# The causal mask of the second key block moved from TensorE to a GpSimd select, and PV one slot later

## The reference

```
x = layernorm(hidden) * ln1_g + ln1_b                 # 32 x 256 x 128
Q, K, V = low-rank projections of x, 16 heads of 8    # each 32 x 16 x 256 x 8
scores = Q @ K^T / sqrt(8)
scores = where(causal, scores, -1e9)                  # query s sees keys t <= s
attn = softmax(scores)
ctx = attn @ V
h = hidden + ctx @ out_U @ out_V + out_b
out = x0 + h + MLP(layernorm(h)) + experts(top 2 of 9)
```

## Time and profile before

| | us |
|---|---|
| median of 3 runs | 999.45 |
| lowest, highest | 994.67, 1008.21 |
| the profiled execution | 1002.02 |
| its span | 1000.1 |

### The profile page before, as it was taken

One profiled execution on the slowest core, in us unless ns is written; L12 is line 12 of the kernel. 1 busy time (PEld: TensorE's weight loads), 2 busy tenths in 40 slices (PEclk: granted clock), 3 DMA queues, 4 the chain that ended last, 5 costly groups with the idle time before them and its releaser, 6 DMA issues. The chain is left out here.

```text
span 1000.1 us, 25308 instructions
## 1 busy us (share of the span) xinstructions
PE 956.2 (96%) x7722; PEld 742.4 (74%) x7722; DVE 698.5 (70%) x3195; ACT 533.9 (53%) x1248; POOL 428.1 (43%) x557
## 2 busy tenths in 40 slices
PE   4689999999999999999999989999999999999997
PEld 4455666666666666666666659999999999989896
DVE  5768889778777777777777745555555554558887
ACT  2663555555555555555555555555555555564442
POOL 9331221354645556454555425444444444430110
PEclk8779999999999999999999999999999999999999
DMA  9477453444554454443433032222222222248874
GB/s 243 126 233 228 164 206 110 136 137 132 156 150 131 126 151 141 130 121 105 134 107 121 30 90 72 66 66 62 66 64 65 65 65 65 73 135 232 230 214 135
DMA packets 139765, 127.12 MB, mean 127 GB/s; under 512 B 17338, under 2 KB 121908, under 8 KB 139636
## 3 DMA queue, kind: packets, MB, share of 16 engines
q1 hardware_dynamic: 116336, 68.94, 25.4%
q0 software_dynamic: 20592, 56.43, 18.0%
q10 hardware_dynamic: 2708, 0.15, 0.2%
HBM read 57.15 MB, written 42.60 MB: 100 GB/s over the span
## 5 line engine op out<-in xcount | busy, mean ns | idle before, releaser
L1441 DVE CUSTOM_DVE_ANT_0 att_masked_st<-att_m_ps,att_mask_st 128x128 bf16<-128x128 f32 (+1 forms) x1024 | 311.4, 353 | 100.1 <-PE att_m_ps L1034 52.1
L846 ACT ACTIVATE att_probs<-att_t_ps 128x512 f32<-128x512 f32 x384 | 229.0, 597 | 206.2 <-PE att_t_ps L1058 201.0
L1683 POOL DMA_INDIRECT y_scratch<-moe_y,moe_row_now x136 | 131.6, 968 | 153.8 <-DVE moe_y L1937 112.6
L664 POOL DMA_INDIRECT slot_x<-xs,att_slot_now x128 | 127.7, 998 | 151.3 <-PE att_t_ps L1058 128.4
L1931 DVE TENSOR_TENSOR moe_hidden<-moe_gate,moe_up_ps 128x352 f32<-128x352 f32 x136 | 70.9, 521 | 109.8 <-ACT moe_gate L1858 108.1
L1058 PE MATMUL att_t_ps<-att_mask_ts,att_ident_b 128*128 128x256 bf16 (+1 forms) x384 | 122.9, 320 | 0.0
L1760 PE MATMUL moe_y_ps<-w_down,moe_hidden_t 128*128 (+1 forms) x816 | 114.0, 276 | 1.7 <-DVE moe_y L1937 1.5
L1858 ACT ACTIVATE moe_gate<-moe_gate_ps 128x352 f32<-128x352 f32 x136 | 63.1, 464 | 97.2 <-PE moe_up_ps L1743 97.2
L1760 PEld LDWEIGHTS moe_y_ps<-w_down,moe_hidden_t 128*128 128x128 f32 (+1 forms) x816 | 101.8, 191 | 3.5 <-issue 3.2
L1441 DVE DVE_READ_ACCUMULATOR2_ANT att_row_max<- 128x1 f32 x1024 | 84.5, 83 | 0.1
L1057 PE MATMUL att_t_ps<-even_stack,att_k_stack 97*128 97x512 f32 x192 | 80.5, 419 | 3.6 <-DMA even_stack<-att_neg_max 3.2
(11 more groups left out here) (268 smaller groups left out, 2053.6 us busy)
## 6 DMA issues: line engine op xcount, KB each, us to landing
att_k_stack<-att_qk_parts POOLq DMA_DIRECT2D x96, 128.0 KB, 3.3
slot_x<-xs POOLq DMA_DIRECT2D x17, 516.0 KB, 3.5
xs<-slot_x SPq DMA_DIRECT2D x34, 258.0 KB, 3.0
xs<-xn_scratch SPq DMA_DIRECT2D x32, 256.0 KB
mlp_rows<-y_scratch POOLq DMA_DIRECT2D x16, 512.0 KB, 5.4
even_stack<-att_qk_parts SPq DMA_DIRECT2D x192, 32.0 KB
att_odd_stack<-att_qk_parts SPq DMA_DIRECT2D x192, 32.0 KB
first_words<-in_L_attn_hidden_states SPq DMA_DIRECT2D x8, 512.0 KB, 7.9
```

Of the source, the lines that this page charges most:

```text
L664: pool.indirect_dma_start(env["slot_x"][:], bass.IndirectOffsetOnAxis(ap=slot_now[c.parity][:, col:col + 1], axis=0), xs[c.parity][:, t, k ...
L846: act.activation(probs[:, m % PT, :], t_ps[m % 2][:], ACT.Exp).then_inc(exp_done, 1)
L1441: last = dve.tensor_tensor_reduce(out=masked_st[m % 2][:, part], in0=m_ps[m % 2][:, part], in1=mask_st[:, SEQ - width:], scale=1.0, scalar ...
L1683: pool.indirect_dma_start(env["y_dram"][:], bass.IndirectOffsetOnAxis(ap=row_now[q.parity][:, t:t + 1], axis=0), y[c.parity][:], None).the ...
```

## The change

Line numbers are those of the kernel before.

1. Score units 8 to 11 of each sequence no longer have the mask matmul (8 of the 24 units of a step). Their probabilities are then wrong above the diagonal until they are zeroed.
2. GpSimd zeroes them in SBUF: a new `keep_causal(c, m)` waits for exp m and runs an `affine_select` in place over 128 x 512 elements, f32, and counts a new semaphore `causal_done`. It is issued twice at the end of pairs 4, 5, 10 and 11 (slots 8 to 11 and 20 to 23), behind what the pair issued before.
3. PV 4, 5, 10 and 11 wait for `causal_done` in place of `exp_done`, and are one slot later: PV 4 in slot 12 (before 11), PV 5 in 14 (before 13), PV 10 in slot 0 of the next step (before 23), PV 11 in slot 2 of the next step (before 1). The others keep their slots.

```
-        scores_done, exp_done = s.sem("scores_done"), s.sem("exp_done")
+        scores_done, exp_done, causal_done = s.sem("scores_done"), s.sem("exp_done"), s.sem("causal_done")
...
+        PV_AT = {3: 0, 5: 1, 7: 2, 9: 3, 12: 4, 14: 5, 15: 6, 17: 7, 19: 8, 21: 9}
+        PV_BEHIND = {0: 10, 2: 11}
... GpSimd
+                def keep_causal(c, m):
+
+                    pool.wait_ge(exp_done, 2 * UNITS * c.index + m + 1)
+                    unit = probs[:, m % PT, :].rearrange("p (i s) -> p i s", i=LANES)
+                    pool.affine_select(out=unit, in_=unit, compare_op=ALU.is_ge, fill=0.0, base=0,
+                                       pattern=[[0, LANES], [1, P]], channel_multiplier=-1).then_inc(causal_done, 1)
...
+                        if 2 * pair % UNITS >= 2 * GROUPS:
+                            keep_causal(p, 2 * pair)
+                            keep_causal(p, 2 * pair + 1)
... TensorE, score_unit
-                    pe.matmul(by_lane, keys, q[rows, g, lanes, queries], start=True, stop=False, skip_group_check=True)
-                    pe.matmul(by_lane[:, :, 0:P], ident_b[:], mask_ts[:, lanes, :], start=False, stop=True, skip_group_check=True).then_inc(scores_done, 1)
+                    last = pe.matmul(by_lane, keys, q[rows, g, lanes, queries], start=True, stop=(u >= 8), skip_group_check=True)
+                    if u < 8:
+                        last = pe.matmul(by_lane[:, :, 0:P], ident_b[:], mask_ts[:, lanes, :], start=False, stop=True, skip_group_check=True)
+                    last.then_inc(scores_done, 1)
... TensorE, probs_times_v
-                    pe.wait_ge(exp_done, 2 * UNITS * c.index + 2 * (n + 1))
+                    if u < GROUPS:
+                        pe.wait_ge(exp_done, 2 * UNITS * c.index + 2 * (n + 1))
+                    else:
+                        pe.wait_ge(causal_done, GROUPS * (2 * c.index + b) + 2 * (u - GROUPS + 1))
... TensorE, step
-                        if slot % 2 == 1 and slot >= 3:
-                            probs_times_v(p, (slot - 3) // 2)
-                        if slot == 1 and not first:
-                            probs_times_v(at(half, d - 1), HALVES - 1)
+                        if slot in PV_AT:
+                            probs_times_v(p, PV_AT[slot])
+                        if slot in PV_BEHIND and not first:
+                            probs_times_v(at(half, d - 1), PV_BEHIND[slot])
...
-                probs_times_v(at(chunks // 2 - 1, 1), HALVES - 1)
+                for n in PV_BEHIND.values():
+                    probs_times_v(at(chunks // 2 - 1, 1), n)
```

## The result

| | before | after |
|---|---|---|
| median of the runs, us | 999.87 (4 runs) | 1034.37 (4 runs) |
| lowest, highest | 994.67, 1008.21 | 1029.39, 1035.35 |
| span of the profiled execution | 1000.1 | 1032.7 |

The changed kernel is slower: the ratio is 1.0342, with an interval of 1.0307 to 1.0377. The forecast was 1007, with a range up to 1018.

The account below looks back on a forecast made before the run. TensorE and the chain of the negated maxima were taken to bound the loop together; 17 free halves at +0.19 and 14 late at +0.26 made +6.9, with the end's -0.2 +6.7 us: 1007 us, range 993 to 1018.

Parts of the forecast that it names:

- What bounds the kernel: Attention loop: TensorE and the chain from turn_max through the maxima's DMA to the score are balanced within 0.17 us.
- Step 1: Masks of slots 8, 9, 20 and 21, ahead of turn_max, go: the chain starts sooner, -0.46 us per half.
- A: As a stretch: slots 8 to 10 and 20 to 22 of a step; 7.38 us before, 6.00 forecast.
- Step 2: Between turn_max and waiting score, masks and first PV go; TensorE waits: -0.07 us per free half, 0 per late one.
- C: As a stretch: slots 12 to 14 and 0 to 2 of a step; 8.20 us before, 9.75 forecast.
- Step 3: The PV moved behind the wait lengthens slot 12 or 0: +0.72 us per half; the other moved PV 0.
- Step 4: GpSimd's eight selects per step, 0.63 us each, hold PV back at most 1.5 us, taken as 0.
- rival C: Selects hold back PV 5 in slot 14 and PV 11 in slot 2: 1033 us; chance 8%.
- Steps 5 and 6: SP's queue and ScalarE: 0; the loop's end, masks gone and last PV waiting for a select: together -0.2 us.
- A (970): Rival: the chain doesn't hold and the masks' 29 us are gained, 970 us; 9% with a partial form at 990.
- B (999): Rival: VectorE sets the pace and absorbs the freed time at its maxima, no change, 999 us; chance 10%.
- B: As a stretch: slots 11 and 23, ending at the score that waits; 3.40 us before, 3.68 forecast.

Follow-up runs that it names:

- e3: Kernel before with the mask matmuls of units 8 to 11 left out, no selects, PV in its old slots: 994.91 us, ratio 0.9948.
- e8: Kernel before with turn_max and copy_max two slots earlier (7 and 19) and SP's stack DMAs split eight and four: 993.29 us, ratio 0.9942.
- e1: Changed kernel with four unneeded matmuls of 512 columns before each score that waits for the negated maxima: 1024.55 us, ratio 1.0248.
- e4: Kernel before with its mask matmuls, no selects, and PV 4, 5, 10 and 11 one slot later: 1023.32 us, ratio 1.0226.
- e6: Changed kernel with SP's twelve query-stack DMAs issued nine before and three behind slot 0's copy of the maxima: 1027.86 us, ratio 1.0294.
- e2: Changed kernel without the GpSimd selects, PV waiting for exp in its new slots: 1031.54 us, ratio 1.0280.
- e5: Changed kernel with PV 4 and 10 back in slots 11 and 23, before the score that waits: 1006.18 us, ratio 1.0072.

## Why the prediction was wrong

**What bounds the kernel: right.** TensorE and the chain of the maxima were balanced, and busy shares did hide it. e3 freed 29 us of TensorE's work and the kernel got 5 us faster; e8 loosened the chain and it got 6 us faster without freeing any.

**Step 1, masks ahead of `turn_max`, right in size:** with the mask of slot 10 (22) A was to fall by 1.38 us per step and fell by 1.33.

**Step 2, the wait: its place and its chain right, its price wrong.** This is the step that failed. The prediction said that TensorE "must wait, in order, and has nothing else to issue", 0.95 us per half; 30 of 31 scores wait, 1.1 us on the mean. The chain from `turn_max` is 3.20 us at slot 12 and 3.44 at slot 0, for 2.93 forecast and 3.33 and 3.30 as the mean of the kernel before. But the wait was priced as its length and 0.10 us of restart. That "the granted clock is full" was read off as a property of the loop, where it is a result of TensorE without holes, which step 2 took away. Measured: C 10.87 with the clock's falls and 9.82 (e1) and 9.81 (e4) without, some 17 us in the loop. The lengths of the waits matter: 0.65 us on the mean in e4 went with one fall in 31 (behind the longest, 1.3 us), 1.1 on the mean (1.5 at the crossing shown) with ten.

The second, smaller error of step 2 is the floor. 2.93 us was the shortest chain, and it was taken for all waits because the median landing is at the least value. At slot 0 it is not: masks of slots 20 and 21 stood between the train's start (1.82 us behind slot 13's score, before and after) and `turn_max`, and without them the copy comes closer behind the train. So a part of step 1's gain is taken back there. e6 shows its size: 3.44 to 3.22 us at one of the two crossings of a step.

**Step 3, the moved PV: right.** +0.72 per half was forecast, from slot 1 and slot 0 as neighbours. e4 has C at 9.81 and e1 at 9.82, for 9.75.

**Step 4 and rival C, GpSimd: right that it doesn't decide.** A select takes 0.667 us, where 0.63 was taken:

```profile
L673 POOL TENSOR_SCALAR_AFFINE_SELECT att_probs<-att_probs 128x512 f32<-128x512 f32 x128 | 82.5, 667 | 15.5 <-ACT att_probs L858 15.0
```

PV waits for it three times, and e2 without it takes the same time. The measured 1034 is the time of rival C (1033) by another way: the number is that of a mechanism which the runs refute.

**Steps 5 and 6: the loop's end mis-sized by 2 us.** Outside the loop the kernel after takes 4.2 us more, where the forecast had -0.2 for the loop's end. From the last score to the first expert matmul it is 10.1 us for 8.3. That goes with the selects and not with the clock or the moved PVs: it is 9.9 to 10.1 in all eight kernels with selects and 8.3 in all six without, e2 and e4 among them, and the clock is full in it before and after (it falls 9.6 and 10.5 us behind the last score). About 0.8 us of it is PVs that end later, 1.2 more idle time ahead of the first expert matmul; what ends that wait was not traced. The rest, experts and MLP, takes 409.0 us for 405.7. The clock is down for 6.8 us at its start, for 3.4 before, which is up to 1.7 us of work; but in kernels that don't differ there this part runs from 403.7 (e1) to 409.0, so that the difference is not shown to be the change's. The stretch ahead of the loop is 0.9 us shorter.

**Rivals A and B.** A (970) needs chains of 1.98 us or less; their means are 3.20 and 3.44. B (999) says that VectorE takes the freed time; it appears with 4.6 us of waits, as a smaller holder behind the first.

**The sum, redone.** +6.7 as forecast; +17 for the clock; +0.17 per step for A and B beyond the forecast, 3 us; +4 outside the loop: +31 of the 32.6 between the spans. The steps that the means leave out hold the rest. In the forecast's own bounds, the lower one (+2 us) has the restart in it all the same; with both terms at their best, as it says, it is about 0. Its estimate of 2.04 us for the transfer, by "Anatomy of one DMA" of the Trainium skill's page "DMA: Bandwidth & Descriptors", has its figure from a section on the path of DMAs that GpSimd issues, while this copy is issued by SP; the sum went by the row (2.1 us), which the kernel after repeats.

## What to carry to other kernels

Before TensorE's time is given back, list each chain of fixed latency between the instruction that starts it and the one that waits for it, and put work that can move in front of the wait, never behind it: here the same four PVs cost 23 us behind it (e4), and two of them back in front recovered 28 us (e5). If an edit opens waits of over 1 us in a dense stretch of TensorE, price them twice, once for their length and once for the clock behind them (here 17 us, beside 22 for the moved PVs), and test the second with matmuls that nothing needs. Starting the chain earlier is the edit that pays (0.6% alone, in e8); "DMA: Bandwidth & Descriptors" of the Trainium skill, section "Rules for kernel authors", says the same: issue early, compute, wait late.

## What the runs showed that was not expected

- In a loop that is otherwise without holes the clock falls behind waits of TensorE of 1.3 to 2.6 us, 0.6 to 1.9 us after work resumed (at 456.8 behind the score at 455.71), and not at every one: nine of the twelve waits for the maxima of over 1.2 us have a fall behind them. In e2 falls came behind waits of 0.9, 1.0 and 1.15 us as well.
- More work made the kernel faster: 128 unneeded matmuls of 512 columns took 9 to 10 us off (e1).
- A DMA of 16 KB whose landing takes 2.1 us at the least, and whose waiting score starts 2.3 us behind the issue when the last of a train on the same queue was issued 2.6 us ahead, takes 2.85 to that score when the train was 2.1 us ahead.
- A GpSimd select in place over 128 x 512 f32 takes 0.667 us, beside a busy VectorE; VectorE's maxima take as long as before (its loop total is 393.5 us against 393.2).
